# A three-layer decoder on one core: a seventh buffer of probabilities, two more in the third layer, and single pieces of the written-out order moved

## The reference

```
x = layernorm(x + proj(attention(x, causal)))            # layer 1
x = layernorm(x + proj(attention(q of x, k and v of ctx, mask)))   # layer 2
x = layernorm(x + attention(x, no mask) + experts(x))    # layer 3
attention: softmax(q k^T / 4 [masked]) v, per head
experts:   gate = softmax(x W_gate + b); combine = the two largest of 8, others 0
           sum over e of (x W_e + b_e) * combine_e       # all eight experts are computed
```

## Time and profile before

| | us |
|---|---|
| median of 3 runs | 916.08 (915.83 to 916.56) |
| the profiled execution | 917.31 |
| its span, first to last instruction | 915.5 |
| PE busy in the span | 875.7 (96%) |
| DVE busy | 767.5 (84%) |
| ACT busy | 587.5 (64%) |
| POOL busy | 427.0 (47%) |
| mean granted TensorE clock | 0.994 |

### The profile page before, as it was taken

The page is one execution under the profiler, slowest core; times in us unless marked ns, Lnnn a source line. Parts: engine busy times, 40 slices in busy tenths (PEclk is TensorE's granted clock), DMA queues, the critical chain, the costliest instruction groups (busy, mean ns, idle before and its releaser), DMA issues.

```text
span 915.5 us, 28485 instructions
## 1 busy us (share of the span) xinstructions
PE 875.7 (96%) x10018; PEld 745.9 (81%) x10018; DVE 767.5 (84%) x3508; ACT 587.5 (64%) x1211; POOL 427.0 (47%) x588
## 2 busy tenths in 40 slices
PE   7899899999999999999999999999999999999996
PEld 4688788888878888888888788888888888888874
DVE  2689787999888988888887888888888888888985
ACT  5578787888867878778787654444555544555533
POOL 7678787898774545445453322222222222222201
PEclk9999999999999999999999999999999999999999
DMA  5665565655544544444343322222222232322200
GB/s 177 171 167 164 142 177 147 165 152 152 150 114 119 149 114 117 129 115 125 107 126 92 80 54 72 83 82 83 83 83 83 82 83 83 83 81 74 78 28 25
DMA packets 98163, 100.47 MB, mean 110 GB/s; under 512 B 10701, under 2 KB 90599, under 8 KB 98023
## 3 DMA queue, kind: packets, MB, share of 16 engines
q1 hardware_dynamic: 98023, 98.66, 38.9%
HBM read 18.14 MB, written 4.19 MB: 24 GB/s over the span
## 4 chain that ended last, share of the span: by engine, by line
PE 73%; issue 7%; DMA 7%; ACT 5%; DVE 4%; SPq 1%; POOL 1%; ACTq 0%; POOLq 0%; DVEq 0%
PE work L515 38%; PE work L659 9%; PE scores L636 8%; PE max_scores L612 7%; DMA q_stack<-neg_max_t 5%; PE work L668 3%; PE scores L639 3%; ACT attn L819 2%; DMA q_stack<-q_parts 1%; PE work L540 1%; DVE max_scores L985 1%; SPq L442 1%; PE work L521 1%; ACT neg_max_t L813 1%; PE work L677 1%
## 5 line engine op out<-in xcount | busy, mean ns | idle before, releaser
L985 DVE CUSTOM_DVE_ANT_0 max_scores<-max_scores,mask_qk 128x128 f32<-128x128 f32 x872 | 223.3, 324 | 37.2 <-PE max_scores L612 37.1
L819 ACT ACTIVATE attn<-scores 128x512 f32<-128x512 f32 x384 | 215.8, 596 | 55.8 <-PE scores L636 49.2
L612 PE MATMUL max_scores<-k_stack,q_stack 126*128 126x128 bf16 x1536 | 145.8, 221 | 6.8 <-DMA q_stack<-q_parts 3.7
L636 PE MATMUL scores<-q_stack,k_stack 128*128 128x128 bf16 x1536 | 141.2, 220 | 11.2 <-DMA q_stack<-neg_max_t 7.7
L612 PEld LDWEIGHTS max_scores<-k_stack,q_stack 126*128 126x128 bf16 x1536 | 98.9, 98 | 40.2 <-issue 19.5
L1099 POOL TENSOR_TENSOR q_full<-q_full,q_parts 128x512 f32<-128x512 f32 x48 | 56.3, 1174 | 152.8 <-ACT q_parts L777 152.8
L1058 DVE SCALAR_TENSOR_TENSOR x_all<-work,combine,x_all 128x256 f32<-128x256 f32 x256 | 121.3, 479 | 6.6 <-PE work L515 1.9
L988 DVE TENSOR_REDUCE neg_max<-max_scores 128x4 f32<-128x512 f32 x166 | 112.3, 680 | 12.8 <-PE max_scores L615 9.9
L985 DVE DVE_READ_ACCUMULATOR2_ANT neg_max<- 128x1 f32 x872 | 122.9, 141 | 0.0
L636 PEld LDWEIGHTS scores<-q_stack,k_stack 128*128 128x128 bf16 x1536 | 96.7, 97 | 30.8 <-DMA q_stack<-neg_max_t 13.8
L515 PE MATMUL work<-split_hi,w_hi 128*128 128x256 f32 x384 | 115.7, 301 | 3.0 <-DVE split_lo L888 2.8
(11 more groups left out here) (125 smaller groups left out, 2098.9 us busy)
## 6 DMA issues: line engine op xcount, KB each, us to landing
k_stack<-k_parts SPq DMA_DIRECT2D x288, 128.0 KB, 2.6
q_stack<-q_parts SPq DMA_DIRECT2D x288, 128.0 KB, 2.5
in_t<-in_xt SPq DMA_DIRECT2D x16, 256.0 KB, 3.1
x_all<-in_x SPq DMA_DIRECT2D x16, 256.0 KB, 3.0
in_t<-in_ct SPq DMA_DIRECT2D x16, 256.0 KB, 3.4
out<-x_all SPq DMA_DIRECT2D x16, 256.0 KB, 2.2
stage<-in_e SPq DMA_DIRECT2D x4, 512.0 KB, 5.1
stage<-in_qk SPq DMA_DIRECT2D x2, 512.0 KB, 4.3
```

The costliest lines, as they stand in the source:

```text
L612: mm = pe.matmul(dst[:, b, h2, :], head(QS, n, 2 * p + h2, b, ROWS), head(KS, n, 2 * p + h2, b, ROWS), start=(b + h2 == 0), stop=(b + h2 = ...
L636: mm = pe.matmul(dst[:, b, h2, :], head(KS, n, 2 * p + h2, b, rows), head(QS, n, 2 * p + h2, b, rows), start=(b + h2 == 0), stop=(b + h2 = ...
L819: act.activation(attn("exp", n, p)[:, :, :], SS[g % 2][:, :, :, :].rearrange("k b h q -> k (b h) q"), ACT.Exp).then_inc(probs_done, 1)
L985: ins = dve.tensor_tensor_reduce(scores, scores, MQ[l][:, :], -1.0, HUGE, ALU.add, ALU.min, NM[n % 2][:, b, h:h + 1])
```

## The change

A seventh `attn` buffer is added. In the third layer two more are used, which are the two input tiles `in_t`: the inputs have all been read by then, and the writer waits for that in the layer's first two items. `SHIFTS` may now name a single piece (`"s24"` is the second scores' piece 4) besides a kind, and the tables have new numbers throughout: `TIMES` of all layers by up to 5 us, in one case 9 (two lines of each stand for them here), and `SHIFTS` for items 0, 1, 2, 14 to 17, 31, 32, 46 and 47. No piece is added or removed, and no instruction computes something else.

```diff
-PERIOD = [16.59, 18.07, 24.92]
+PERIOD = [16.59, 18.07, 24.9]
...
-     "s2": [-1.13, -1.06, 2.2, 2.6, 9.76, 11.14, 11.59, 14.48],
+     "s2": [-1.56, -0.65, 2.13, 2.26, 9.08, 11.5, 11.74, 14.65],
...
+def shift(n, name):
+    return SHIFTS.get(n, {}).get(name, 0.0)
...
-ORDER = sorted([(base(n) + t + SHIFTS.get(n, {}).get(kind, 0.0), kind, n, part) for n in range(NITEM)
+ORDER = sorted([(base(n) + t + shift(n, kind) + shift(n, f"{kind}{part}"), kind, n, part) for n in range(NITEM)
...
-ATTN_BUFS = 6
+ATTN_BUFS = 7
+MORE_BUFS = 2
...
-        j = min((i for i in range(ATTN_BUFS) if free_at[i] <= t), key=lambda i: free_at[i])
+        j = min((i for i in range(ATTN_BUFS + (MORE_BUFS if layer(n) == 2 else 0)) if free_at[i] <= t), key=lambda i: free_at[i])
...
         def attn(kind, n, part):
-            return AT[ATTN_SLOT[(kind, n, part)]]
+            j = ATTN_SLOT[(kind, n, part)]
+            if j < ATTN_BUFS:
+                return AT[j]
+            return IN[j - ATTN_BUFS][:, :, :].rearrange("p c (k q) -> p (c k) q", k=4 // C)

         def attn_free(eng, kind, n, part):
+            if ATTN_SLOT[(kind, n, part)] >= ATTN_BUFS and turn(n) <= 2:
+                eng.wait_ge(ch_done, NSTEP)
+                eng.wait_ge(cl_done, NSTEP)
```

More of the change, by code:

```diff
@@ L60 @@
 RB_COLS = 2 * D + E
-PERIOD = [16.59, 18.07, 24.92]
+PERIOD = [16.59, 18.07, 24.9]
 TIMES = [
[4 rows of a table removed]
-     "max": [-18.73, -18.28, -13.85, -12.08, -10.39, -8.09, -5.87, -4.3], "nm": [-3.92], "maxt": [-3.48],
[4 rows of a table removed]
-     "norm": [31.53], "causal": [2.74, 3.79, 3.8, 4.61, 6.05, 8.11, 9.52, 10.06], "va": [-15.89]},
[4 rows of a table removed]
-     "max": [-16.75, -15.08, -14.32, -12.04, -11.47, -8.29, -8.01, -6.18], "nm": [-5.99], "maxt": [-2.95],
[9 rows of a table removed]
-     "max": [-26.31, -24.84, -23.6, -21.09, -16.38, -15.43, -13.63, -11.69], "nm": [-7.43], "maxt": [-6.94],
[3 rows of a table removed]
-     "gtop": [-19.6], "gateT": [-15.09], "cbt": [-16.2], "bias": [-14.46], "eb": [-15.47],
-     "expert": [-8.01, -6.29, -4.28, 0.9, 3.15, 5.51, 7.24, 13.17],
-     "combine": [-6.82, -4.36, -2.79, 1.34, 4.29, 5.8, 9.19, 14.67], "zadd": [13.03, 22.61], "stat": [25.94],
-     "rs": [20.03], "norm": [32.29], "store": [27.66]},
[4 rows of a table added]
+     "max": [-18.99, -18.31, -14.09, -11.97, -10.4, -8.58, -5.87, -5.05], "nm": [-3.81], "maxt": [-3.36],
[4 rows of a table added]
+     "norm": [30.54], "causal": [3.05, 4.1, 4.4, 4.92, 7.33, 8.46, 9.68, 10.37], "va": [-16.2]},
[4 rows of a table added]
+     "max": [-16.76, -15.11, -14.5, -12.26, -12.01, -8.19, -8.02, -6.19], "nm": [-6.13], "maxt": [-3.8],
[9 rows of a table added]
+     "max": [-26.3, -24.92, -22.49, -20.47, -16.42, -15.16, -13.82, -11.58], "nm": [-7.33], "maxt": [-6.6],
[3 rows of a table added]
+     "gtop": [-19.74], "gateT": [-15.14], "cbt": [-15.74], "bias": [-13.77], "eb": [-14.48],
+     "expert": [-7.53, -6.25, -4.44, 1.13, 3.05, 5.52, 7.38, 13.39],
+     "combine": [-6.34, -4.53, -2.95, 1.57, 4.19, 5.81, 9.49, 14.89], "zadd": [12.7, 22.32], "stat": [26.4],
+     "rs": [20.16], "norm": [32.16], "store": [27.32]},
 ]
 SHIFTS = {
[9 rows of a table removed]
[11 rows of a table added]
 }
@@ L210 @@
 BANK, BANK_BEFORE = assign_banks()
-ATTN_BUFS = 6
+ATTN_BUFS = 7
+MORE_BUFS = 2
 def assign_buffers():
     slot, before = {}, {}
-    free_at, last = [-1e9] * ATTN_BUFS, [None] * ATTN_BUFS
+    free_at, last = [-1e9] * (ATTN_BUFS + MORE_BUFS), [None] * (ATTN_BUFS + MORE_BUFS)
     for t, kind, n, part in ORDER:
```

## The result

| | before | after |
|---|---|---|
| median, same chip | 916.32 (915.83 to 918.65) | 924.28 (923.8 to 925.74) |
| the profiled execution's span | 915.5 | 922.5 |
| mean granted TensorE clock | 0.994 | 0.989 |

The medians are of four runs each and lie 8.0 us apart. The ratio of after to before, taken over the runs, is 1.0074, with a 95% interval of 1.0055 to 1.0094; that is 6.8 us, with 5.0 to 8.6. I had forecast 913.1 us with a range up to 917.2; the sign was wrong.

What follows compares the result with a forecast made beforehand. PE was taken to bound the kernel, busy 875.7 of 915.5 us. Start 0.7, first layer 0.7 less 0.6, borders 1.2 and 0.2, third layer 0, end 0.8 gave 3.0 us won: 913.1 us, range 910.3 to 917.2.

Steps and rivals of the forecast that it cites:

- The third layer, predicted 0: Third layer: `xt` moves, scores swap places, PE starts pieces at the same distances; delay stays inside the margin, 0 us.
- my third rival: Third layer: later `xt`, `xh`, `xl` and first `max` make `maxt` wait in every item; 5.2 us, time 918.3, chance 0.13.
- the margin of 0.53 us at `nm` and `maxt`: Third layer: `nm` ends at 725.42, `maxt` starts at 725.95; this 0.53 us was to absorb `xl`'s delay of up to 0.3.
- The contention that I weighed for `xl`: Third layer: POOL's `ql` overlapping DVE's two-input `xl` would lengthen one of them; nothing of it would reach PE.
- Item 5, predicted 0.7 won: Item 5's first `s1`: earlier `ql` and weights halve PE's 1.50 us wait for `q_stack`; 0.7 us won, bounds 0 and 1.5.
- The first layer, predicted 0.6 lost over eight items: Items 4 to 12: `xh` ahead of `va` delays the first `exp` and fourth `s2`; 0.08 us per item, 0.6 lost.
- First to second layer, predicted 1.2 won: First border: new order takes away two of PE's waits, may add one; 1.2 us won, bounds 2.8 won and 1 lost.
- Second to third layer, predicted 0.2 won: Border to the third layer: its stretch has less idle time than the first border; 0.2 us won.
- The start, predicted 0.7 won: Item 0: earlier `maxt`, with `q` and `v` filling PE's wait before the first `s2`; 0.7 us won.
- the bound of 0.5 lost: Start: the lower bound of its term, a loss of 0.5 us from `xh` placed ahead of `qe` and `qh`.
- The end, predicted 0.8 won: Last item: last `zT` 1.3 us earlier, last `zadd` at 907.8 instead of 908.62; 0.8 us won, between 0 and 1.4.
- The buffers, predicted nothing: Additional buffers: take away ACT's waits for a free buffer, hidden by PE's products; costed at nothing.

Runs made afterwards that it cites:

- first_s1_ahead: Kernel after, but in the third layer each item's first `s1` stands ahead of the first `s2` again; ratio to the kernel before 1.0017.
- weights_late: Kernel after, but the second load of weights is issued behind the last of item 5's q and k stacks; ratio to the kernel before 1.0039.
- four_taken_back: Kernel after with third-layer first `s1`, `xh` of items 5 to 13 and a `w_hi` put back, second weights load behind item 5's stacks; 0.9989 of before.
- new_end_late_weights: Kernel before with nine buffers, items 46 and 47 placed as after, second weights load behind item 5's stacks; ratio to the kernel before 0.9991.
- before_again: The unchanged kernel before, timed and profiled once more on another chip; ratio to itself 1.0019.
- after_again: The unchanged kernel after, timed and profiled once more on the same chip as the repeated kernel before; ratio to the kernel before 1.0062.

## Why the prediction was wrong

- **The third layer, predicted 0.** This is the failed step that no run disputes: +1.96 us from item 33 to 45, or 0.11 to 0.16 per item over both pairs, and 0.6 to 1.1 more from item 45 to 46. I had the mechanism as my third rival, a first `max` that comes later and a DVE without slack behind it, and dismissed it by the margin of 0.53 us at `nm` and `maxt`. That margin is real (from item 33 to 45 `maxt` starts some 0.5 us behind `nm` in both kernels and waits for it nowhere), but it was not the first to be used up. Ahead of it stands the bank of the first `pv`, which had a margin of nothing: before, `pv` was issued 0.26 us behind the `combine`. And I looked at `xt`: its `xh` did come 0.75 us later, as forecast, and `xl` 0.16. Neither can be what costs, since first_s1_ahead keeps `xt` behind `v` and has the value of before. The piece was the first `s1`, which I passed over as "the scores swap places". The contention that I weighed for `xl` isn't there either: in this layer it reads one of its two inputs from PSUM (`split_lo<-work,split_hi`), and it took 0.68 us in both kernels.
- **Item 5, predicted 0.7 won.** I took an earlier `ql` and an earlier load for an earlier stack. The load now stands ahead of the last `k` stack too, and the wait grew: by 0.5 us in the first pair, to 1.3 to 2.5 in later profiles against 0.9 to 1.5. weights_late shows that the load in front of the stacks makes the wait; that its move by one place made it longer fits the profiles and was not tried by itself. The low clock behind it, 1.3 us more, I had considered at the start only.
- **The first layer, predicted 0.6 lost over eight items.** 0.9 to 1.0 lost from 6 to 12. The term was nearly right in size and wrong in kind: `xh` gave 0.2 on item 5, ahead of this stretch, and 0.3 on item 9; 0.6 was `w_hi` behind `norm`, a move that I had not priced.
- **First to second layer, predicted 1.2 won.** 0.5 to 0.8 lost in the two pairs (78.0 and 78.4 against 77.5 and 77.6). The waits of `maxt` that I had counted did go or shrink: at item 15 it was 0.75 us and is none, at item 16 it went from 0.8 to 0.2. But from item 12 to 14 it takes 1.2 to 1.3 us longer in each kernel with this order (29.2 against 27.9). I had counted waits that might go, not those that come; what makes the items 12 and 13 longer was not followed further.
- **Second to third layer, predicted 0.2 won.** Nothing that can be seen without a low clock (59.44 to 60.00 us against 59.25 to 60.20 with the order of before), although the wait of `gateT` is 0.6 to 0.8 us longer; 2.3 us lost in the first pair, with one.
- **The start, predicted 0.7 won.** Nothing, by fifteen profiles. That `s2` would wait for nothing was right; that the chain to it stays at 3.2 us was wrong, and the bound of 0.5 lost held.
- **The end, predicted 0.8 won.** To the last `zadd` it was right, step by step: 0.83 us, and the last `zT` 1.25 earlier where I had 1.3. To the end of the program it was wrong: only 0.14 us are left, since the last store lands 0.7 us later, and no term of mine stood behind the `zadd`.
- **The buffers, predicted nothing.** For PE's waits this held: four_taken_back and new_end_late_weights have all nine. But each kernel that has them pays the 0.4 to 0.9 us in the last store; that the buffers are the reason is likely and not shown.

The two pairs of profiles add up as follows. The first pair's stretches are in the table of the result and give the 7.0 us of its span. The second (before_again to after_again, on one chip) is 4.6 us: 0.3 at the start, 0.9 at 4 to 6, 0.9 at 6 to 12, 0.8 at 12 to 17, 0.1 in the second layer, 0.7 won at the second border (where before_again had the low clock), 1.4 in the third layer, 1.0 at 45 to 47 and 0.1 won behind it. What both pairs have is 0.9 to 2.0 (items 4 and 5), 0.9 to 1.0 (first layer), 0.5 to 0.8 (first border), 1.4 to 2.0 (third layer) and 0.5 to 1.0 (45 to 47), less 0.1 at the end: 4.1 to 6.7 us, where the ratios give 5.7 (0.0062) and 6.8 (0.0074). The rest is low clock and the landing of transfers, which change from one profile to the next. What stays open is the loss from item 12 to 14, and why the last pieces from 46 to 47 vary (21.8 to 22.5 us).

## What to carry to other kernels

Where one engine runs a list without a gap for most of a period, find every place where another engine waits for it, bank reuse included, and take the smallest margin, not that of the wait you know; the wait may be filed under another releaser. A move at the head of such a list is paid in each period, if one of these margins is nothing: here one of 0.23 us cost 0.11 to 0.16 us. Follow the chain to the last instruction of the program, and not to the last piece that was moved. And before a gain or a loss at one place is explained from a pair of profiles, profile the same kernel again: with the order of before the start varied by 2.8 us and the second layer by 3.4, the third layer by 0.1 (with the new order by 0.5).

## What was not expected of the hardware

- The granted clock fell to 0.50 behind a wait of PE of 1.4 us in one execution and stayed at 1.00 behind the same or a longer wait in another; where it fell at the border to the third layer, the stretch took 1.5 us more in the mean with the new order (61.3 against 59.7) and 1.1 more with that of before.
- Adding 3.5 us of products to PE did not lengthen the kernel after (1.0035 against 1.0062 and 1.0074 of before).
- The last store took 2.15 to 2.16 us to land in three profiles, and 2.57 to 3.04 in the twelve in which a transfer of 8 KB of instructions fell into it.
